# One drain on GpSimd behind each unit of sixteen indirect gathers

## What is computed

```python
sim = einsum("pbnhd,pkhd->pbnhk", q, pk_keys)          # two halves of a key, 64 each
scores, idx = top_k(sim, 16)
index = idx[0][..., :, None] + idx[1][..., None, :] * 64   # 256 candidates
final_scores, pk_idx = top_k(score, 16)
ind = take_along_axis(index, pk_idx) + head * 4096
k = einsum("bnhk,bnhkd->bnhd", softmax(final_scores), keys_table[ind])
v = einsum("bnhk,bnhkd->bnhd", softmax(final_scores), values_table[ind])
```

## Time and profile before

| | us |
|---|---|
| runs, median of 3 | 8802.18 (8794.76 to 8821.96) |
| span of the profiled execution | 12370.4 |
| busy in it: PE / VectorE / ScalarE / GpSimd | 7191.2 / 5008.5 / 3309.2 / 5931.2 |
| granted TensorE clock in it, mean share | 0.566 |
| gathers | 6144, of 964 ns on average |

### The profile page before, as it was taken

How to read it: one execution, slowest core, us unless ns; L and a number is a source line. 1 busy time by engine, 2 the same in 40 slices (tenths; PEclk the granted TensorE clock), 3 DMA queues, 4 the chain that set the end, 5 groups by cost and what they waited for, 6 DMA issues and landing times.

```text
span 12370.4 us, 121689 instructions
## 1 busy us (share of the span) xinstructions
PE 7191.2 (58%) x34736; PEld 5456.4 (44%) x34736; DVE 5008.5 (40%) x16213; ACT 3309.2 (27%) x9869; POOL 5931.2 (48%) x6158
## 2 busy tenths in 40 slices
PE   7758665665756657566665756647576565424103
PEld 5456454443545435454354544435454444313102
DVE  1243625345253442524435253352534435352612
ACT  1112222223222232222322223222222223222222
POOL 0044445455454454544445454454545545565663
PEclk7655655555555555555655555555555555555555
DMA  1011111111111111111111111111111111111111
GB/s 27 7 41 37 35 39 41 38 38 41 36 42 40 40 38 37 41 41 39 36 38 45 36 42 38 37 41 40 39 40 41 39 38 41 41 41 39 41 47 28
DMA packets 658255, 472.33 MB, mean 38 GB/s; under 512 B 557990, under 2 KB 558494, under 8 KB 657183
## 3 DMA queue, kind: packets, MB, share of 16 engines
q0 software_dynamic: 196608, 403.05, 12.7%
q1 hardware_dynamic: 460896, 60.59, 3.1%
HBM read 461.04 MB, written 2.10 MB: 37 GB/s over the span
## 4 chain that ended last, share of the span: by engine, by line
PE 29%; another core or an unknown queue 27%; issue 18%; DVE 16%; DVEq 4%; ACT 4%; SPq 1%; DMA 1%; POOL 0%; ACTq 0%; POOLq 0%
PE MM L438 5%; DVE KV L876 3%; PE PB L1134 2%; PE PB L1107 2%; ACT GATH L869 2%; PE PB L1172 2%; PE PB L1148 1%; PE PB L1162 1%; PE PB L1131 1%; PE MM L390 1%; DVEq L851 1%; DVE I L814 1%; PE MM L453 1%; DVE PF L852 1%
## 5 line engine op out<-in xcount | busy, mean ns | idle before, releaser
L645 POOL DMA_INDIRECT GATH<-in_table,IDX x6144 | 5925.4, 964 | 6313.4 <-DVE KV L876 3824.1
L869 ACT ACTIVATE GATH<-GATH,WT 128x128 f32<-128x128 f32 x6144 | 1907.1, 392 | 237.8 <-issue 236.8
L438 PE MATMUL MM<-SPEC,SW 128*128 128x8 f32 (+1 forms) x8800 | 1259.7, 297 | 863.1 <-issue 420.6
L876 DVE TENSOR_REDUCE KV<-GATH 128x128 f32<-128x2048 f32 x384 | 1391.0, 3622 | 691.7 <-ACT GATH L869 354.1
L438 PEld LDWEIGHTS MM<-SPEC,SW 128*128 128x128 f32 (+1 forms) x8800 | 1266.8, 264 | 864.4 <-issue 862.5
L506 ACT ACTIVATE U<-MM 128x320 f32<-128x320 f32 (+1 forms) x416 | 219.1, 527 | 1882.2 <-remote 988.1
L547 DVE COPY TURN<-TP 80x512 f32<-80x512 f32 (+1 forms) x512 | 347.1, 684 | 925.4 <-remote 391.8
L390 PE MATMUL MM<-F,TURN 128*128 128x80 f32 x2048 | 436.7, 384 | 464.7 <-DVE TURN L547 345.9
L506 ACT ACTIVATE SPEC<-MM 128x160 f32<-128x160 f32 x320 | 96.1, 300 | 2068.2 <-remote 1283.4
L390 PEld LDWEIGHTS MM<-F,TURN 128*128 128x128 f32 x2048 | 404.5, 292 | 535.1 <-issue 278.6
L477 PEld LDWEIGHTS MM<-G,TURN 80*128 80x128 f32 x2048 | 343.5, 240 | 507.1 <-DVE TURN L547 239.0
(11 more groups left out here) (202 smaller groups left out, 11494.3 us busy)
## 6 DMA issues: line engine op xcount, KB each, us to landing
GATH<-in_table,IDX POOLq DMA_INDIRECT x6144
SW<-in_sw SPq DMA_DIRECT2D x1280, 40.0 KB
CONV<-in_cwb SPq DMA_DIRECT2D x128, 4.0 KB
CONV<-in_cwb SPq DMA_DIRECT2D x128, 0.1 KB
U<-in_xT SPq DMA_DIRECT2D x16, 96.0 KB
out<-OUTB SPq DMA_DIRECT2D x16, 96.0 KB
W1E<-in_w SPq DMA_DIRECT2D x1, 520.0 KB
W2E<-in_w SPq DMA_DIRECT2D x1, 512.0 KB
```

What stands on the lines that cost most here:

```text
L438: m = e.matmul(pv[r, :, k, :], SW[r, half, k % HM, w:w + WID * beside], Sv[r, :, c * MODES + k, :], start=True, stop=True)
L645: e.indirect_dma_start(GATH[:, r, k, :], None, table, bass.IndirectOffsetOnAxis(IDX[:, u // H, u % H, k:k + 1], 0)).then_inc(gath[r], 16)
L869: m = e.activation(GATH[:, r, k, :], GATH[:, r, k, :], ACT.Copy, scale=WT[:, u // H, u % H, k:k + 1])
L876: e.tensor_reduce(KV[:, u // H, u % H, :], GATH[:, u % RING, :, :].rearrange("p k d -> p d k"), AX.X, ALU.add).then_inc(S["gather_free"], 1)
```

## The change

`pool_gather` gets a `drain()` on GpSimd behind the sixteen gathers of each unit. Nothing else differs; lines behind 645 are numbered one higher.

```diff
@@ -643,6 +643,7 @@
                 fence(e)
                 for k in range(TOPK):
                     e.indirect_dma_start(GATH[:, r, k, :], None, table, bass.IndirectOffsetOnAxis(IDX[:, u // H, u % H, k:k + 1], 0)).then_inc(gath[r], 16)
+                e.drain()
```

## The result

The changed kernel takes **9736.45 us** (median, 9730.0 to 9740.79) against 8798.47 of the kernel before: a ratio of 1.1061, with a 95% interval of 1.1038 to 1.1085. That is 938 us slower; 9630 was predicted, inside a range of 8930 to 10,700.

The account below looks back on a forecast made before the run. GpSimd was taken to bound the runs almost without a pause. Each of 383 borders costs 1.9 + 0.1 + 0.8 - 0.3 = 2.5 us, so 8802.2 + 957.5 - 130 = 9630 us, range 8930 to 10,700.

Parts of the forecast that it names:

- The bound: GpSimd bounds the runs almost without a pause: 8542.7 us of its own, at most 259.5 us of waits.
- Run-ahead and restart: At each border, 0.1 us from drain to next gather and 0.8 us restart, less today's 0.3 us gap.
- The tail: From a unit's last gather's end to the drain's end: 1.9 us, taken between 1.3 (data landed) and 2.5.
- The cover: GpSimd's remaining waits at borders swallow part of the drains: half of 259.5 us, 130 us.
- a drain that ends with the descriptors: Rival: the drain at a border ends once the last gather's descriptors are made, tail about nothing: 8940 us, 12%.
- The full tail of 5.3 us: Rival: every border has the 5.3 us tail of the drain at the program's end: 10,930 us, 8%.
- Hidden: Rival: gathers take less in a run, GpSimd is not the bound and the drain is hidden: 8802 us, 8%.
- faster: Rival: drains end bursts after one unit, so the other engines start again sooner: 8660 us, 3%.
- The profiled span: The changed kernel's profiled span should rise by no more than 140 us, or even fall.
- other engines are slower in a profiled execution: Explanation for the span of 12370.4 us against runs of 8802.18: PE's instructions fall away while gathers run on.

Follow-up runs that it names:

- the second profile: The kernel before, unchanged, profiled once more: the run took 8778.04 us, its span is 8776.2 us.
- e4: Kernel before plus one small fill on GpSimd behind each unit, with no wait that holds anything: 8858.82 us, ratio 1.0072.
- e5: Kernel before plus, behind each unit, a wait until its sixteen gathers have landed and then a drain: 10008.67 us, ratio 1.1372.
- e8: Kernel before plus, behind each unit, a GpSimd wait until the last gather's descriptors are made, no drain: 9031.47 us, ratio 1.0265.
- e1: Kernel before plus, behind each unit, a GpSimd wait until its sixteen gathers have landed, no drain: 9575.59 us, ratio 1.0886.

## Why the prediction was right

- **The bound.** Right, and by the sum on which everything stood: span less waits of GpSimd, 8542.7 us, left at most 259.5 us of waits in a run; the second profile shows 231.2. In the changed kernel GpSimd waits for almost nothing but its own drains. e4 qualifies it: added time on GpSimd arrives only once some 100 us of waits are filled. Beyond that it does arrive: from the changed kernel to e5 a border grew by 0.77 us, 293 us over 383, and 267 more were measured over before.
- **Run-ahead and restart.** Right in size: 0.1 + 0.8 us were priced, 0.106 + 0.777 measured, and the 0.3 fell away as said.
- **The tail.** This is the term that was mis-sized: 1.9 us against 2.21, which by itself is 383 x 0.31 = 119 us, more than the 106 by which 9630 missed. The reason given for it was wrong: its upper end, 2.5 us, was read from the standstill of the other engines behind a burst, and in the second profile, whose span agrees with the runs, there is no such standstill. What stands in its place is the landing, 1.2 us to the last packet, and 1.03 us more until the drain is through. That the value came near is luck.
- **The cover.** 130 us were taken; it is 107 between the two profiles and 1074 - 938 = 136 by the medians of the runs.
- **The rivals.** No border is under 2.96 us, so a drain that ends with the descriptors is out; e8 shows what it would have cost, 228 us, where 138 was the price given (8940). The full tail of 5.3 us is real, but goes with 64 gathers on the list and not with 16; that it might come from three units in one burst was the right doubt with the wrong cause. Hidden and faster are out with the 938 us, and with GpSimd's 47% of the chain.
- **The profiled span.** That it would move by at most 140 us up, or fall, said nothing: it fell by 2631 us because the first profile of the kernel before was unlike its runs. The step that failed is the sentence that other engines are slower in a profiled execution (and PE did not fall to none in the earlier trace rows; one instruction is left): two profiles of one kernel differ by 3594 us, and the spans of all other kernels here agree with their runs.

## What to carry to other kernels

When span and runs disagree, subtract what the suspected bound waits for from the span and hold the rest against the runs; if it comes out just below, that engine is the bound, and nearly every microsecond put on it arrives once its last waits are filled. A drain on GpSimd behind indirect gathers is not a sequencer's trifle: it waits for the data to land (tail of 2.21 us behind 16 gathers), takes 0.08 us for each gather since the last drain, and keeps the sequencer from queueing the next ones. Where a wait is needed, a semaphore for the descriptors made cost 0.58 us a border, but doesn't tell that the data are there; one for the data landed cost 2.15, against 2.80 for the drain. Both semaphores leave the pause of 1.2 us at every 80th gather, 0.24 us a unit, which a drain behind each unit takes away.

## What the runs showed that was not expected

- A drain's own work on GpSimd grows by 0.0817 us for each gather since the last drain (1.344 us behind 16, 7.877 behind 96, all landed), and is smaller again behind 128 or more (3.97 us of tail behind 128, 5.27 and 5.30 us behind 144 and 6144).
- Where no drain stands between and GpSimd has no gather queued, one gap grows from 0.30 to some 1.5 us every 80 gathers, first ahead of the 114th (76 times in e8 and in e1).
- One profiled execution of the kernel before took 12370.4 us where another took 8776.2 and the runs 8776 to 8822, with the same gathers (964 and 967 ns) and the same gap of 0.30 us, but with the other engines standing still while gathers ran on the earlier trace rows. Its page puts 27% of the chain down to another core or an unknown queue, which no other page here does. No run here repeated it, and its cause stays open.
